# Weighted sums of the attention in groups of 8, 8 and 9 key tiles in place of 4, with a ring of eight places for the exponentials in place of four

## The reference

```python
def _L1_attn_ref(x, Wq, bq, Wk, bk, Wv, bv):
    q = jnp.einsum('bsd,de->bse', x, Wq) + bq
    k = jnp.einsum('bsd,de->bse', x, Wk) + bk
    v = jnp.einsum('bsd,de->bse', x, Wv) + bv
    scores = jnp.einsum('bqd,bkd->bqk', q, k) / jnp.sqrt(jnp.asarray(d, x.dtype))
    attn = jax.nn.softmax(scores, axis=-1)
    out = jnp.einsum('bqk,bkd->bqd', attn, v)
    return out + x
...
t = t + _L1_attn_ref(_ln_t(t), L1_attn_Wq, ...)      # t: 16 images x 3136 positions x 32
```

## Time and profile before

| | |
|---|---|
| median of 3 runs | 3477.34 us (3470.15 to 3479.36) |
| the profiled execution | 3478.2 us |
| its span, first to last instruction | 3476.4 us |
| mean granted TensorE clock | 0.953 |
| TensorE (PE) busy | 3097.7 us, 89% |
| VectorE (DVE) busy | 2478.3 us, 71% |
| ScalarE (ACT) busy | 2240.6 us, 64% |
| GpSimd (POOL) busy | 620.3 us, 18% |

### The profile page before, as it was taken

The page is one execution under the profiler, slowest core; times in us unless marked ns, Lnnn a source line. Parts: engine busy times, 40 slices in busy tenths (PEclk is TensorE's granted clock), DMA queues, the critical chain, the costliest instruction groups (busy, mean ns, idle before and its releaser), DMA issues.

```text
span 3476.4 us, 66176 instructions
## 1 busy us (share of the span) xinstructions
PE 3097.7 (89%) x23337; PEld 1393.9 (40%) x23337; DVE 2478.3 (71%) x3210; ACT 2240.6 (64%) x3889; POOL 620.3 (18%) x497
## 2 busy tenths in 40 slices
PE   3898998889986899999999999999999999999775
PEld 2555555555553433333333333333333333333354
DVE  6677777777773777787787777777777777777342
ACT  2466666666664567776776776776776776777520
POOL 0344444444442010110010010010010011011100
PEclk6899999999998899999999999999999999999976
DMA  3000000000002701011001001101101101100022
GB/s 81 3 13 14 14 14 10 13 14 14 14 9 91 261 1 20 1 20 20 10 11 21 19 3 21 20 1 21 20 1 21 20 1 21 20 1 1 7 32 43
DMA packets 130462, 81.72 MB, mean 24 GB/s; under 512 B 111284, under 2 KB 120085, under 8 KB 129173
## 3 DMA queue, kind: packets, MB, share of 16 engines
q1 hardware_dynamic: 128629, 78.26, 9.2%
q10 hardware_dynamic: 1568, 0.04, 0.0%
HBM read 39.57 MB, written 32.11 MB: 21 GB/s over the span
## 4 chain that ended last, share of the span: by engine, by line
PE 76%; DVE 10%; issue 5%; ACT 4%; DMA 2%; POOL 1%; ACTq 1%; DVEq 0%; SPq 0%; POOLq 0%
PE ps L1517 17%; PE ps L1494 14%; PE ps L1464 14%; PE ps L1293 8%; DVE arena L1116 6%; PE ps L1318 3%; PE ps L1285 2%; PE ps L1347 2%; ACT arena L686 2%; PE ps L1527 2%; PE ps L1353 2%; PE ps L1306 2%; PE ps L1476 1%; DMA arena<-in_x 1%; PE ps L1333 1%
## 5 line engine op out<-in xcount | busy, mean ns | idle before, releaser
L1116 DVE TENSOR_REDUCE arena<-ps 128x2 f32<-128x896 f32 (+1 forms) x1408 | 1485.3, 1083 | 454.5 <-PE ps L1464 440.9
L799 ACT ACTIVATE arena<-ps 128x512 f32<-128x512 f32 (+1 forms) x2464 | 1377.9, 595 | 549.3 <-PE ps L1494 539.0
L1494 PE MATMUL ps<-arena 97*128 97x512 f16 (+1 forms) x2800 | 896.9, 360 | 23.5 <-issue 18.9
L1464 PE MATMUL ps<-arena 96*128 96x448 f16 x2800 | 774.4, 359 | 35.9 <-DVE arena L1116 27.0
L1517 PE MATMUL ps<-arena 128*32 128x512 f32 (+1 forms) x6176 | 683.7, 520 | 17.6 <-DVE arena L1138 17.0
L1494 PEld LDWEIGHTS ps<-arena 97*128 97x128 f16 (+1 forms) x2800 | 255.5, 100 | 704.6 <-ACT arena L799 464.1
L1464 PEld LDWEIGHTS ps<-arena 96*128 96x128 f16 x2800 | 256.4, 99 | 321.9 <-DVE arena L1116 108.2
L1293 PE MATMUL ps<-arena 128*49 128x196 f32 x2048 | 295.7, 340 | 55.7 <-ACT arena L686 52.4
L576 POOL TENSOR_TENSOR tok<-arena,tok 128x128 f32 (+3 forms) x112 | 48.0, 429 | 1583.0 <-DVE arena L1138 1583.0
L517 POOL TENSOR_TENSOR arena<-arena 113x784 f32<-113x784 f32 x128 | 192.7, 1506 | 485.2 <-DVE arena L966 485.2
L1293 PEld LDWEIGHTS ps<-arena 128*49 128x49 f32 x2048 | 199.7, 125 | 160.6 <-ACT arena L686 55.7
(11 more groups left out here) (178 smaller groups left out, 2875.0 us busy)
## 6 DMA issues: line engine op xcount, KB each, us to landing
arena<-qk_scratch SPq DMA_DIRECT2D x96, 196.0 KB, 4.1
qk_scratch<-arena SPq DMA_DIRECT2D x16, 448.0 KB, 4.8
arena<-ximg SPq DMA_DIRECT2D x16, 400.0 KB, 7.0
arena<-in_x SPq DMA_DIRECT2D x4, 1568.0 KB, 8.4
xa_scratch<-arena SPq DMA_DIRECT2D x32, 196.0 KB, 1.9
res_scratch<-arena SPq DMA_DIRECT2D x32, 196.0 KB, 2.0
arena<-xa_scratch SPq DMA_DIRECT2D x4, 1568.0 KB, 8.9
arena<-res_scratch SPq DMA_DIRECT2D x4, 1568.0 KB, 12.5
```

The source lines that it names most:

```text
L799: act.activation(pk[0:rows, x % DEPTH, QC * m:QC * m + n], ps[0:rows, w % SB, 0:n], ACT.Exp, scale=float(C) ** -0.5).then_inc(att["exp"], 1)
L1116: dve.tensor_reduce(mxp[0:rows, p, 2 * u:2 * u + k], ps[0:rows, at_:at_ + k, 0:KN], AX_X, ALU.max)\
L1464: last = pe.matmul(ps[0:rows, MB + 2 * (j % 2) + n % 2, 0:KN], q2[p][0:96, T * t:T * t + rows], k2[p][0:96, KN * m:KN * m + KN], start=Tru ...
L1494: last = pe.matmul(ps[0:rows, bank, at_ % QC:at_ % QC + chunk_cols(c)], k2[p][0:97, T * t:T * t + rows], q2[p][0:97, QC * c:QC * c + chunk ...
```

## The change

The weighted sums of a chunk of 512 queries are made in three groups in place of seven. Before, after every second step the two steps' four key tiles were summed, and the last key tile by itself. Now four steps (eight key tiles) are summed after the steps in which the fourth, and the eighth, have become due, and the last five steps (nine key tiles) together. The chunk of 64 queries is summed as before. The ring `pk` gets eight places in place of four. It then reaches beyond 4S, so the tile `lnq` moves behind it, and ScalarE waits for the transfers out of `hl` before its first instruction of the attention. The order of the groups' last steps, and with it the copy of the sums and the output product, stays where it was.

```diff
-DEPTH = 4
+DEPTH = 8
...
         lnc = carve(NT * C).rearrange("p (t c) -> p t c", t=NT)
-        assert at[0] <= 4 * S
-        at[0] = 4 * S
         lnq = carve(NT * C).rearrange("p (t c) -> p t c", t=NT)
+        assert at[0] <= 6 * S
         at[0] = 6 * S
...
             y = x - LAG
             k = (y + (NSTEP if y < 0 else 0)) - first_of[steps2[y][0]]
+            if steps2[y][0] == NQ - 1:
+                return [y - 1, y] if k % 2 else []
             if k == NT // 2:
-                return [y]
-            return [y - 1, y] if k % 2 else []
+                return list(range(y - k % 4 - 4, y + 1))
+            return [y - 3, y - 2, y - 1, y] if k % 4 == 3 and k + 1 < NT // 2 else []
...
+            act.wait_ge(prep["stored_a"], 64 * G)
+            act.wait_ge(prep["stored_b"], 64 * G)
             max_row(0, 0, 0, 0)
             image_steps(0, 0, first=True)
```

## The result

The changed kernel takes 3497.29 us in the median of five runs (3495.73 to 3502.38), the kernel before 3477.34 (3470.15 to 3480.34): a ratio of 1.0063 with a 95% interval of 1.0048 to 1.0078. It is slower by 0.6%, some 20 us. The forecast was slower by 38 us, to 3515. The measured time lies inside the range that was to hold eight in ten (3450 to 3545) and 3 us under the forecast's own narrower range (3500 to 3532): the sign and the mechanism hold, the size was forecast at about twice what was measured.

What follows compares the result with a forecast made beforehand. TensorE was taken to set the pace, coupled to VectorE by a ring of two pair jobs. Stretch losses of 2.4 us an image over 16 images made 38 us slower, 3515 us; range 3500 to 3532, eight in ten 3450 to 3545.

Steps and rivals of the forecast that it cites:

- The group's fixed cost: TensorE leaving for a burst of weighted sums and coming back: 0.247 us, 24 fewer groups an image, 95 us in all.
- steps 2 to 5: Stretch of a chunk holding the output product: 7.10 us with five jobs, against 7.18 before, a gain of 0.08.
- Plain stretch: Four steps with four pair jobs between bursts: 5.50 us against 5.46 before, as VectorE sets the burst's start.
- ScalarE's ring: Ring of three scores: holds the seventh score tile of a plain stretch by 0.24 us once VectorE's reductions are cut.
- Rows of maxima: Stretches with a row of maxima in the last step: 6.27 against 6.15, loss 0.12; 7.27 against 6.85, loss 0.42.
- The layer norm's stretches: Stretches with VectorE's sum, 8.63 against 7.56, loss 1.07, and squares' sum, 7.23 against 6.37, loss 0.86.
- the other twelve: Remaining stretches of an image's 18: each between a gain of 0.27 and a loss of 0.33, together within 0.1 of zero.
- The ring, ScalarE's wait, the moved tile at nothing: The larger ring, ScalarE's wait for stored queries and keys, and the moved tile lnq were all costed at nothing.
- The idle time of TensorE behind the pair ring: Sign in the profile after: TensorE's idle time ahead of L1464, released by VectorE, grown to several hundred us.
- The faster one: Rival: waits don't come, 95 us kept, 3383; sign: plain stretch's J4 starts under 2.9 us; chance 0.19, whole or part.
- No change: Rival: only the layer norm's two stretches lose, 1.93 us, the other sixteen gain 0.12 each: 3478 within 10; chance 0.18.
- The clock's fall: Rival: new idle times in the layer norm's two stretches drop TensorE's clock, 96 us more, 3612; chance 0.05.

Runs made afterwards that it cites:

- both cuts: VectorE's maxima over half the keys and ScalarE's exponentials over half the queries: changed kernel 3311.69 us; groups of before with the ring of eight 3374.16 us.
- e5: The changed kernel with VectorE reducing only the first 224 of each 448 columns of the pair jobs: 3326.34 us.
- the ring alone: The changed kernel (ring of eight, moved tile, ScalarE's wait for the stores) with the groups of before: 3475.88 us, ratio 1.0001 to the kernel before.

## Why the prediction was right, and where it was off

- *The group's fixed cost, 0.247 us.* Right where it can be seen alone: 0.24 to 0.28 for one group fewer in steps 2 to 5 with both cuts. As a sum of 95 us it was too high, since the 64-key tile's change of shape (0.11), the squares' sum and the way over mq had been covered by bursts that are gone. With both engines made cheap 62 us are left.
- *Plain stretch 5.50.* Measured 5.51. Both rings are read right: the hand-over of 0.06, the spacing of 1.00 on VectorE. ScalarE's ring, put at 0.24 us of wait where VectorE doesn't bind (e5), is worth 5.43 - 5.21 = 0.22.
- *Rows of maxima, losses of 0.12 and 0.42.* Measured 6.28 - 6.15 = 0.13 and 7.27 - 6.85 = 0.42.
- *The layer norm's stretches, losses of 1.07 and 0.86.* Measured 1.05 and 0.86. That the cover is gone is shown by moving the two reductions away: the new groups gain some 21 us more by it than the old ones.
- *The term that was mis-sized: steps 2 to 5.* I had one at a gain of 0.08 and the others within a sum of zero. The five in one image gain 0.26, 0.16, 0.23, 0.26 and 0.16, together 1.08 us. Of the first, with a forecast of 7.10 and 6.92 measured, the trace shows the last pair 4.37 us after the stretch begins, where 7.10 would need 4.55; the working that gave 7.10 isn't written out, so which step of it was long stays open. Of the other twelve one loses 0.35 (steps 10 to 14 of the fifth chunk), a little beyond the bound of 0.33, and together they gain 0.46, not zero. The stretches from step 6 of an image to step 74 sum to 110.84 - 108.77 = 2.07 us lost, and steps 75 to 5 of the next gain 0.29. So an image loses 1.8 in place of 2.4.
- *A term that was not in the sum: the loop's boundary.* The loop has seven passes, so it goes back to its start six times. From step 75 of the last image of a pass to step 6 of the next image the kernel took 22.3 to 25.2 us before and takes 21.2 to 22.1 after, 1.86 less in the mean, where 0.29 was gained between other images. TensorE after, at the third of them:

```profile
2119.25 2.14 PE L1520 MATMUL ps<-arena 128*32 128x512 f32 x24
2123.51 0.38 PE L1497 MATMUL ps<-arena 97*128 97x512 f16 x1 [2.12 <-issue]
```

  The idle time here was 3.14 us and is 2.12, with a burst of nine tiles as TensorE's last work before it. But over all six boundaries TensorE's idle time is the same, 21.5 and 21.4 us, as more of it now comes ahead of the output product that follows. What falls is the time TensorE is busy with the same matmuls, from 120.2 to 109.1 us, since it spends less of it at the lower clock. The windows view of the fourth boundary, before and after (columns as in the earlier trace rows):

```profile
2362.40:2387.60 25.20, 21.64 (x171) 9.29 (x168) 11.63 (x16) 12.91 (x24) 0.70 (x2) 0.73 0.35 65
2374.20:2396.10 21.90, 18.53 (x170) 8.98 (x166) 11.28 (x14) 12.41 (x24) 0.70 (x2) 0.84 0.23 54
```

  Over the six, the granted clock is 0.73 to 0.85 before and 0.84 to 0.92 after. Why it comes back sooner no run separates. The forecast had no term for this. Without it the loss would be 16 x 1.8 = 29 us, so about half of the forecast's miss lies here. The whole sum is 16 x 2.07 - 9 x 0.29 - 6 x 1.86 = 19.3 us, and 1.6 for a fall of the clock (below) make 20.9. Step 75 of the last image begins 20.9 us later in the trace after; the two profiled spans differ by 19.1.
- *The ring, ScalarE's wait, the moved tile at nothing.* Right, shown by the ring alone.
- *The idle time of TensorE behind the pair ring.* I had looked for several hundred us; the waits view has 66.0, up from 27.0. My own sum didn't give several hundred either: 95 us saved and 38 lost make 133 us of waits. The matmuls' ends are modelled, so a wait of 0.1 or 0.2 lies within the tail of the matmul before and isn't counted as idle. The start times show it, the waits view does not: the fourth pair of the plain stretch above is held until 2.96 us, and its row has no idle time before it.
- *The rivals.* The faster one fell with the plain stretch: its fourth pair starts at 2.96, not under 2.9. The Trainium skill's rule that a change of the tiling mode drains TensorE (TensorEngine Tiling (Array Packing), Key Properties) agrees with a group's fixed cost of 0.247 us, but says nothing of who waits afterwards. *No change* needed the sixteen stretches beside the layer norm's two to give back 1.93 us an image; they gave 0.13. The clock's fall is the rival that came true in one place: over two images the windows view has 0.99 as before, with idle times up to 0.90 and 1.4 us, but in the squares' sum stretch of image 14 (counted from 0) the clock fell right after the idle time of 1.41 us. Timeline of TensorE and windows view after:

```profile
3088.72 0.38 PE L1479 MATMUL ps<-negid,mq 128*1 128x128 f16 x4 [1.41 <-DVE mq L1126]
...
3089.96 3.52 PE L1520 MATMUL ps<-arena 128*32 128x512 f32 x16
```

```profile
3090.00:3094.00 4.00, 4.00 (x20) 0.87 (x20) 0.94 (x1) 0.95 (x3) 3.76 (x2) 0.57 0.00 0
```

  The burst took 3.52 in place of 1.92 us and the stretch 8.83 in place of 7.23. In the profiled execution the same stretch kept its clock in all other images, after idle times of 1.3 to 1.4 us, so the price was 1.6 us and not 96. Why this one fell stays open.

## What to carry to other kernels

In this kernel a long run of matmuls saved its fixed switching cost only where the engines on short rings behind TensorE were not late afterwards. Price such a run by what they can't be fed in that time, and follow one stretch with start times rather than mean busy shares. A burst also covers things (a reduction of another stage, the way from a last reduction to the matmul that needs it, a change of shape), so when bursts are merged, list what each one covered and move that first. Here that, and long bursts only where they paid, turned a loss of 20 us into a version 49 us faster than the kernel before.

## What was not expected of the hardware

A score tile with 64 keys between tiles of 128 costs TensorE 0.22 us (0.65 against 0.43, new groups with both cuts), 0.11 of it on the way out (0.34 against 0.23, old groups with both cuts). That is nearly as much as leaving for a burst of weighted sums and coming back (0.25). Behind such a burst the way in is free: 0.99 us from the burst's start, as for a full tile.

An idle time of 1.41 us was followed by a fall of the granted clock once, and by none in the other images, where it was 1.34 to 1.41 us. At the loop's boundary, with an idle time of 1.8 to 2.2 us and a second one of 0.7 to 1.6 us soon after, the clock fell all six times.
